# The experts' second product turned round: weights on the loaded side, in 64-column tiles

## The chip, the cores and the metric

One core of a Trainium2 chip runs the whole program, two transformer-like layers with a mixture of experts in the first. The metric is device time in microseconds, the median of several executions. The change touches one stage of it, the experts' two products.

## The reference, cut to what matters

```python
E, S, D, M = (48, 4, 256, 256);  K = D // S          # K = 64
def _L0_ffn_ref(x, Wr, W1, b1, W2, b2):
    xf = x.reshape(-1, D)                             # 4096 rows
    cap = int(CAP_FACTOR * T / E)                     # 128
    vals, idx = jax.lax.top_k((xf @ Wr.T).T, cap)
    w = jax.nn.softmax(vals, axis=-1)
    xg = xf[idx]
    h = jax.nn.gelu(jnp.einsum('ecd,esdm->ecsm', xg, W1) + b1[:, None], approximate=False)
    y = jnp.einsum('ecsm,esmk->ecsk', h, W2) + b2[:, None]
    y = y.reshape(E, cap, D) * w[..., None]
    out = jnp.zeros_like(xf).at[idx.reshape(-1)].add(y.reshape(-1, D))
```

Each of 48 experts takes 128 of the 4096 rows. In each of its four splits it multiplies them by a 256 x 256 matrix, applies gelu, and multiplies by a 256 x 64 matrix. The four results side by side make 256 columns. They get the bias b2, are weighed per row, and are added back at the rows they came from. Everything here is fp32.

## The kernel before

The stage is the second half of `expert_choice`. Each engine has its own program, a loop over the 48 experts e, and semaphores join them. The orders are written out by hand.

**SP** loads the weights into a ring of 8 slots: `load_expert` issues W1 (1024 KB), W2 (256 KB) and b2, which it spreads over all 128 partitions (128 KB). The loads of expert e+8 go out when `y_biased` says that add(e) is done.

**POOL** runs `scatter(e)`, then `gather(e+5)` (LEAD is 5), then waits until scatter(e-1) has landed and raises `y_free`. `scatter(e)` waits for `y_ready`, which weigh(e) raises. A gather is an indirect DMA of 128 rows of 1 KB, a scatter the same with an addition.

**TensorE**, in iteration e, runs up(e+1), turn(e+2), at some experts a small product for the list search (`pick_ps`), and down(e).
- `turn` transposes the gathered rows `xg` into `x_ps`, two transposes (L1216).
- `up` is the first product, 16 matmuls in the code (L1225), with loaded weights of 128 columns and 128 streamed columns.
- `down` is the second product (L1236). The loaded side is `act_h` (128 rows of the expert as columns), the streamed side is w2 with 64 columns:

```python
for s in range(S):
    cols = slice(s * KS, (s + 1) * KS)
    for c in range(KD):
        last = pe.matmul(y_ps[:, e % 2, cols], act_h[:, e % 2, s * KD + c, :], w2[:, e % RING, s, c, :], ...)
```

Each fp32 product of the code is two matmuls in the profile, and a transpose is one, so up has 32 records per expert, down 16 and turn 2.

**ScalarE**, in iteration e, runs gelu(e+1) (eight activations, L942), weigh(e) (L949) and x_copy(e+3) (L936). At e = 8 and e = 24 it also runs `exps`, one exponential for the list search (L953), for which it loads another table and then the gelu table again.

**VectorE** runs add(e) (L1106), which adds b2 to `y_ps`, and at about half of the experts pieces of the list search for later experts: rounds of top-8, a sort, counts and shifts.

PSUM has eight banks. x_ps takes one, h_ps four, y_ps (two buffers) one, and pick_ps two.

Of the kernel before, what the change touches and what calls it, by code (L numbers as in the profile page):

```python
# [12 lines left out]
ALU = mybir.AluOpType  # L13
ACT = mybir.ActivationFunctionType
# [6 lines left out]
P = 128  # L21
B, N, D = 4, 1024, 256
# [3 lines left out]
KD = D // P  # L26
# [4 lines left out]
KS = D // S  # L31
# [41 lines left out]
def columns(ap):  # L73

    return ap.rearrange("(c p) -> p c", p=P)
# [522 lines left out]
def expert_choice(nc, mk, g, a):  # L598

    with ExitStack() as ctx:  # L600
        t = Maker(nc, ctx)
        w1 = t.sb("w1", [P, RING, S, KD, M])
        w2 = t.sb("w2", [P, RING, S, KD, KS])
        b2_rows = t.sb("b2_rows", [P, RING, D])
        b1T = t.sb("b1T", [P, E * S, KD])
        index = t.sb("index", [P, E], U32)
        weight = t.sb("weight", [P, E])
# [6 lines left out]
        def load_expert(eng, e, q):  # L614

            eng.dma_start(w1[:, q], a["L0_ffn_W1"][bass.ds(e, 1)].rearrange("a s (p k) m -> p (a s) k m", k=KD)).then_inc(w_in[q], 16)
            eng.dma_start(w2[:, q], a["L0_ffn_W2"][bass.ds(e, 1)].rearrange("a s (p k) n -> p (a s) k n", k=KD)).then_inc(w_in[q], 16)
            eng.dma_start(b2_rows[:, q, :], a["L0_ffn_b2"][bass.ds(e, 1)].rearrange("a s n -> (a s n)").partition_broadcast(P)).then_inc(w_in[q], 16)

        lists_in = [mk.sem("lists_in0"), mk.sem("lists_in1")]  # L620
        proj2 = t.sb("proj2", [MF, 2, DH])
# [173 lines left out]
        with ExitStack() as c2:  # L795
# [3 lines left out]
            xg = t.sb("xg", [P, XG, D])  # L799
            xT = t.sb("xT", [P, 2, KD, P])  # L800
            act_h = t.sb("act_h", [P, 2, S * KD, P])
            y, biased_y = t.sb("y", [P, 2, D]), t.sb("biased_y", [P, 2, D])
            x_ps = t.ps("x_ps", [P, 2, D])
            h_ps = t.ps("h_ps", [P, 2, S * KD, P])
            y_ps = t.ps("y_ps", [P, 2, D])
            pick_ps = t.ps("pick_ps", [P, 2, 512])
            fold_ps = h_ps[:].rearrange("p q c n -> p (q c n)")

            top, at, at_f = t.sb("top", [P, CAP]), t.sb("at", [P, CAP], U32), t.sb("at_f", [P, CAP])
# [17 lines left out]
                mk.sem("slot_set"), mk.sem("xg_turned"), mk.sem("xT_ready"), mk.sem("up_done"),  # L827
                mk.sem("gelu_done"), mk.sem("down_done"), mk.sem("y_ready"))
            added = [mk.sem("added_even"), mk.sem("added_odd")]
            carried, y_free, y_biased = mk.sem("pool_carried"), mk.sem("y_free"), mk.sem("y_biased")  # L830
            mod_in, cols_in, w2_summed = mk.sem("mod1_in"), mk.sem("cols_in"), mk.sem("w2_summed")
            fold_turned, fold_copied, fold_done, fold_ready, blank = (
                mk.sem("fold_turned"), mk.sem("fold_copied"), mk.sem("fold_done"), mk.sem("fold_ready"), mk.sem("features_blank"))
# [10 lines left out]
            with nc.Block() as block:  # L844
                @block.sync
                def _(sp):
                    for e in range(FOLD_SLOT):
                        load_expert(sp, e, e)
                    sp.dma_start(g.b1_elu[:], columns(a["L1_attn_b1"]), allow_slow_non_contiguous=True).then_inc(cols_in, 16)
                    for i, name in enumerate(("ln1_g", "ln1_b")):  # L850
                        sp.dma_start(g.ln1_col[:, i, :], columns(a[f"L1_attn_{name}"]), allow_slow_non_contiguous=True).then_inc(cols_in, 16)
                    mod_columns = g.mod_dram[1].rearrange("b (s k p) -> s k p b", s=6, k=KD)
                    for k in range(KD):
                        sp.dma_start(g.gain_col[:, k, :], mod_columns[CB, k], allow_slow_non_contiguous=True).then_inc(cols_in, 16)
                        sp.dma_start(g.shift_col[:, k, :], mod_columns[SB, k], allow_slow_non_contiguous=True).then_inc(cols_in, 16)
                    for i, name in enumerate(("b1", "quantum_phases", "quantum_weights_real", "quantum_weights_imag")):
                        sp.dma_start(g.wav[:, i, :], columns(a[f"L1_ffn_{name}"]), allow_slow_non_contiguous=True).then_inc(cols_in, 16)
                    for i in range(2):
                        sp.wait_ge(fold_out[i], 16)
                        load_expert(sp, FOLD_SLOT + i, FOLD_SLOT + i)  # L860
                    sp.dma_start(mod[:, :, 0:GB, :], g.mod_dram[1].rearrange("b (s d) -> b s d", s=6)[:, 0:GB, :].partition_broadcast(P)).then_inc(mod_in, 16)
                    sp.wait_ge(elu_consts, 1)
                    for e in (ELU_SLOT, ELU_SLOT + 1):
                        load_expert(sp, e, e)
                    sp.wait_ge(wave_consts, 1)
                    load_expert(sp, WAVE_SLOT, WAVE_SLOT)
                    for e in range(E - RING):
                        sp.wait_ge(y_biased, e + 1)
                        load_expert(sp, e + RING, e % RING)
                    sp.wait_ge(mod_in, 16)  # L870
# [62 lines left out]
                def _(act):  # L933
# [10 lines left out]
                        last.then_inc(gelu_done, 1)  # L944

                    def weigh(e):
                        act.wait_ge(y_biased, e + 1)
                        act.wait_ge(y_free, e + 1)
                        act.activation(y[:, e % 2, :], biased_y[:, e % 2, :], ACT.Copy, scale=weight[:, e:e + 1]).then_inc(y_ready, 1)  # L949

                    def exps(p):
                        act.wait_ge(edge_ready, p + 1)
                        act.activation(ex[:], top[:], ACT.Exp, bias=edge[:, 1:2]).then_inc(top_exp, 1)  # L953
# [15 lines left out]
                    act.activation(g.elu_const[:], fold_ps[:, 0:CF], ACT.Copy)  # L969
                    act.activation(g.w2_sum[:], fold_ps[:, 512:512 + D], ACT.Copy)  # L970
                    act.wait_ge(wave_consts, 1)
                    act.activation(g.wave_const[:].rearrange("p c b -> p (c b)"), fold_ps[:, 1024:1024 + CF * B], ACT.Copy).then_inc(consts_out, 1)
                    exps(0)
                    act.sem_inc(y_ready, 2)
# [4 lines left out]
                    for e in range(E):  # L979
                        if e + 1 < E:  # L980
                            gelu(e + 1)
                        weigh(e)
                        if e + 3 < E:
                            x_copy(e + 3)
                        if e == COUNTS_AT[1]:
                            exps(1)
                        if e == COUNTS_AT[2]:
                            exps(2)

                @block.vector  # L990
                def _(dve):
# [14 lines left out]
                    def turn_back(p):  # L1006
                        dve.wait_ge(top_turned, p + 1)
                        v(dve.tensor_copy(topT[:].rearrange("p (q e) -> p q e", e=EP), of_pair(pick_ps[:, 1, 0:P], 1)))
                        dve.sem_inc(topT_ready, 1)
                        v(dve.tensor_copy(kept[:], pick_ps[0:HALF, 0, 0:P]))  # L1010

                    def sort(rows):

# [89 lines left out]
                    def add(e):  # L1103
                        dve.wait_ge(down_done, e + 1)
                        dve.wait_ge(y_ready, e + 1)
                        dve.tensor_tensor(biased_y[:, e % 2, :], y_ps[:, e % 2, :], b2_rows[:, e % RING, :], ALU.add).then_inc(y_biased, 1)  # L1106

                    v(dve.tensor_reduce(by_expert[:], g.ident[:].rearrange("p (n e) -> p e n", e=EP), AX.X, ALU.add))
                    v(dve.tensor_copy(same[:].rearrange("p (n e) -> p n e", e=EP), by_expert[:].unsqueeze(1).to_broadcast([P, LISTS, EP])))
# [63 lines left out]
                def _(pe):  # L1173
# [43 lines left out]
                        last.then_inc(turned, 1)  # L1217

                    def up(e):
                        pe.wait_ge(w_in[e % RING], 48 * (e // RING + 1))  # L1220
                        pe.wait_ge(xT_ready, e + 1)
                        for s in range(S):
                            for c in range(KD):
                                for k in range(KD):
                                    last = pe.matmul(h_ps[:, e % 2, s * KD + c, :], w1[:, e % RING, s, k, c::KD], xT[:, e % 2, k, :],  # L1225
                                                     start=(k == 0), stop=(k == KD - 1))
                        last.then_inc(up_done, 1)

                    def down(e):
                        pe.wait_ge(gelu_done, e + 1)  # L1230
                        if e:
                            pe.wait_ge(y_biased, e)
                        for s in range(S):
                            cols = slice(s * KS, (s + 1) * KS)
                            for c in range(KD):
                                last = pe.matmul(y_ps[:, e % 2, cols], act_h[:, e % 2, s * KD + c, :], w2[:, e % RING, s, c, :],  # L1236
                                                 start=(c == 0), stop=(c == KD - 1))
                        last.then_inc(down_done, 1)

                    pe.wait_ge(proj_in, 32)  # L1240
                    pe.transpose(fold_ps[:, 0:MF], proj2[:].rearrange("m i d -> m (i d)"), g.ident[0:MF, 0:MF]).then_inc(fold_turned, 1)
# [26 lines left out]
                    pe.wait_ge(wave_w_in, 16)  # L1268
                    for c in range(CF):
                        for k in range(KD):  # L1270
                            last = pe.matmul(fold_ps[:, 1024 + c * B:1024 + (c + 1) * B], w_wave[:, k, c * P:(c + 1) * P], g.shift_col[:, k, :],
                                             start=(k == 0), stop=(k == KD - 1))
                    last.then_inc(wave_consts, 1)
                    turn_top(0)
                    send_lists(0)
# [10 lines left out]
                    for e in range(E):  # L1286
                        if e + 1 < E:
                            up(e + 1)
                        if e + 2 < E:
                            turn(e + 2)  # L1290
                        for p in range(1, PHASES):
                            if e == COUNTS_AT[p] - 4:
                                turn_top(p)
# [12 lines left out]
                            if e == COUNTS_AT[p] + 5:  # L1306
                                join_weights(p)
                        down(e)
        mk.clear_signals()


# [1288 lines left out]
```

## Time and profile before

| | us |
|---|---|
| median of 3 executions (1674.59 to 1681.48) | 1678.65 |
| span of the profiled execution | 1681.8 |
| first up of the expert stage starts | 232.85 |
| last scatter of the expert stage is issued | 526.78 |
| TensorE busy, whole span | 1508.4 |
| DMA, whole span | 158.23 MB, mean 94 GB/s |

The span runs from the first to the last instruction of the profiled execution; it is one execution, so it need not be the median. A row of the timeline merges neighbours of one kind: it gives the start, the time to the end of the last, and their number. Matmuls overlap each other in the records: one of 0.27 us may be followed by the next 0.11 us later, so rates are read from starts. A time "to landing" runs from a DMA's issue to its last byte.

### The profile page before, as it was taken

The numbers are of one execution on the slowest core, as the hardware profiler recorded it, in microseconds if no ns is written. First come the engines' busy times: TensorE is split into PE (matmuls) and PEld (weight loads), VectorE is DVE, ScalarE is ACT, GpSimd is POOL, SyncE is SP. The second block draws the span as 40 slices with busy tenths as digits, with TensorE's granted clock in tenths as the row PEclk, the third lists the DMA queues.
The fourth block names the chain that finished last, engine by engine and source line by source line (L and its number), as shares of the span: only waits on it lengthen the run. The fifth ranks groups of instructions, "written<-read, shape, count | busy, mean of one in ns | idle before, by whom it ended". The sixth has DMA issues, their size and how long they took to land. (4 is left out here: it accounts for less than half of the span.)

```text
span 1681.8 us, 23213 instructions
## 1 busy us (share of the span) xinstructions
PE 1508.4 (90%) x8509; PEld 1261.0 (75%) x8509; DVE 1169.0 (70%) x2251; ACT 697.7 (41%) x1289; POOL 532.7 (32%) x520
## 2 busy tenths in 40 slices
PE   8876759999994699999987999999987899989997
PEld 7443649999994566666645888888866789979996
DVE  6674786674001778787638778787856888899996
ACT  1044124545442222222222333333326767767774
POOL 2412025555552022222314000000004555556666
PEclk9877569999997799999997999999998999999999
DMA  5545829999973101111013000000013100000001
GB/s 200 226 137 170 277 69 291 278 293 273 290 217 94 52 26 62 51 38 38 25 50 113 1 25 26 26 26 25 13 34 120 51 13 26 1 1 26 14 26 38
DMA packets 128624, 158.23 MB, mean 94 GB/s; under 512 B 14336, under 2 KB 96376, under 8 KB 127488
## 3 DMA queue, kind: packets, MB, share of 16 engines
q1 hardware_dynamic: 115296, 135.80, 24.9%
q0 software_dynamic: 9216, 12.59, 3.7%
q10 hardware_dynamic: 4000, 8.37, 1.4%
q8 instruction: 67, 1.10, 0.3%
q14 instruction: 45, 0.37, 0.1%
HBM read 122.35 MB, written 33.60 MB: 93 GB/s over the span
## 5 line engine op out<-in xcount | busy, mean ns | idle before, releaser
L2234 POOL TENSOR_TENSOR ff_hid_lo<-ff_hid,ff_hid_hi 128x512 fp32r<-128x512 f32 x128 | 172.7, 1353 | 148.2 <-ACT ff_hid_hi L2143 146.8
L1225 PE MATMUL h_ps<-xT,w 128*128 128x128 f32 x1536 | 192.9, 284 | 1.1 <-ACT xT L936 1.1
L1225 PEld LDWEIGHTS h_ps<-xT,w 128*128 128x128 f32 x1536 | 186.3, 197 | 1.7 <-issue 1.7
L2522 PE MATMUL ff_down<-ff_w_hi,ff_hid_hi 128*128 128x256 f32 x512 | 147.3, 288 | 7.6 <-POOL ff_hid_lo L2234 4.5
L2523 PE MATMUL ff_down<-ff_w_lo,ff_hid_hi 128*128 128x256 f32 x512 | 145.6, 284 | 0.0
L2524 PE MATMUL ff_down<-ff_w_hi,ff_hid_lo 128*128 128x256 f32 x512 | 145.6, 284 | 0.0
L116 POOL TENSOR_TENSOR ff_rstd<-ff_var,minus_half 128x4 f32<-128x4 f32 x24 | 26.0, 1083 | 360.3 <-DVE ff_var L111 356.2
L1106 DVE TENSOR_TENSOR biased_y<-y_ps,b_rows 128x256 f32<-128x256 f32 x48 | 20.4, 424 | 156.1 <-PE y_ps L1236 152.2
L1319 PE MATMUL k_ring<-w_hi,hT_hi 128*128 128x512 f32 x256 | 118.3, 462 | 9.9 <-DVE hT_lo L1479 6.4
L1660 PE MATMUL k_acc<-wide_rows,hk 128*128 128x512 f32 x256 | 119.6, 599 | 4.1 <-ACT wide_rows L1604 4.1
L1319 PE MATMUL q_ring<-w_hi,hT_hi 128*128 128x512 f32 x256 | 109.8, 429 | 8.8 <-PEq L99 6.8
L1949 PE MATMUL q_out_ps<-kv_sums,wide_rows 128*128 128x256 f32 x512 | 115.5, 379 | 0.0
L2522 PEld LDWEIGHTS ff_down<-ff_w_hi,ff_hid_hi 128*128 128x128 f32 x512 | 98.7, 193 | 14.8 <-POOL ff_hid_lo L2234 6.8
L1595 ACT ACTIVATE k_squares<-k_ring 128x1024 f32<-128x1024 f32 x32 | 32.8, 1025 | 182.0 <-PE k_ring L1321 182.0
L2508 PE MATMUL ff_ring<-ff_rowsT_hi,ff_w_hi 128*128 128x512 f32 x256 | 102.8, 402 | 4.6 <-DVE ff_hid L2328 2.8
L1949 PEld LDWEIGHTS q_out_ps<-kv_sums,wide_rows 128*128 128x128 f32 x512 | 96.3, 190 | 13.2
L942 ACT ACTIVATE act_h<-h_ps,b1T 128x128 f32<-128x128 f32 x384 | 104.2, 391 | 2.7 <-PE h_ps L1225 2.7
L1321 PE MATMUL k_ring<-w_hi,hT_lo 128*128 128x512 f32 x256 | 102.0, 399 | 0.0
L2509 PE MATMUL ff_ring<-ff_rowsT_lo,ff_w_hi 128*128 128x512 f32 x256 | 102.0, 399 | 0.0
L1320 PE MATMUL k_ring<-w_lo,hT_hi 128*128 128x512 f32 x256 | 101.9, 398 | 0.0
L2523 PEld LDWEIGHTS ff_down<-ff_w_lo,ff_hid_hi 128*128 128x128 f32 x512 | 98.9, 193 | 4.1
L1321 PE MATMUL q_ring<-w_hi,hT_lo 128*128 128x512 f32 x256 | 101.8, 398 | 0.0
(419 smaller groups left out, 3683.5 us busy)
## 6 DMA issues: line engine op xcount, KB each, us to landing
w<-in_L_ffn_W_dram SPq DMA_DIRECT2D x48, 1024.0 KB, 5.8
w<-in_L_ffn_W_dram SPq DMA_DIRECT2D x48, 256.0 KB, 6.0
expert_sum_dram<-f_zero SPq DMA_DIRECT2D x8, 1024.0 KB, 15.1
b_rows<-in_L_ffn_b_dram SPq DMA_DIRECT2D x48, 128.0 KB, 8.3
x<-in_L_attn_x_dram SPq DMA_DIRECT2D x4, 1024.0 KB, 12.0
h_dram<-hg SPq DMA_DIRECT2D x8, 512.0 KB, 3.0
hk<-expert_sum_dram SPq DMA_DIRECT2D x8, 512.0 KB, 4.2
hT_hi<-expert_sum_dram SPq DMA_DIRECT2D x8, 512.0 KB, 4.9
```

What stands on the lines that cost most here:

```text
L942: last = act.activation(act_h[:, e % 2, s * KD + c, :], h_ps[:, e % 2, s * KD + c, :], ACT.Gelu, bias=b1T[:, e * S + s, c:c + 1])
L1225: last = pe.matmul(h_ps[:, e % 2, s * KD + c, :], w1[:, e % RING, s, k, c::KD], xT[:, e % 2, k, :], start=(k == 0), stop=(k == KD - 1))
L1319: pe.matmul(out, x[0], w[0][:, cols], start=start, stop=False)
L1321: return pe.matmul(out, x[1], w[0][:, cols], start=False, stop=stop)
L1660: last = pe.matmul(acc[:, k, cols], hk[:, n % KV_RING, j, k * P:(k + 1) * P], dash[:, n % 2, j, cols], start=(j == 0), stop=(j == G - 1))
L1949: last = pe.matmul(out_ps[:, i % 2, 0:D], qnT[:, i % 2, c, :], kv_out(i // TB)[:, c, :], start=(c == 0), stop=(c == CH - 1))
L2234: pool.tensor_tensor(hid_lo[:, m % PARTS, :], hid[:, m % WHOLES, :], hid_hi[:, m % PARTS, :].bitcast(F32), ALU.subtract).then_inc(part_low, 1)
L2508: pe.matmul(slot(u), high[:, d, cols], x[:, n % 2, d, :], start=(d == 0), stop=False)
L2509: pe.matmul(slot(u), high[:, d, cols], x_low[:, n % 2, d, :], start=False, stop=False)
L2522: pe.matmul(into, hid_hi[:, m % PARTS, tile], high[:, c, :], start=(c == 0 and j % 2 == 0), stop=False)
L2523: pe.matmul(into, hid_hi[:, m % PARTS, tile], low[:, c, :], start=False, stop=False)
L2524: last = pe.matmul(into, hid_lo[:, m % PARTS, tile], high[:, c, :], start=False, stop=(c == CF - 1 and j % 2 == 1))
```

## The change

- The second product is turned round. The loaded side is now w2, 64 columns; the streamed side is `act_h`, 128 columns. The result `yT_ps` is transposed: splits 0 and 1 of a pair lie in partitions 0 to 63 and 64 to 127, and the two pairs side by side. In program order neighbours alternate between the two halves.
- b2 lies along partitions then. It is loaded once (`b2_rows`, 48 x 256), transposed by two small products at the start and copied to `b2T`. The 48 loads that spread b2 are gone, and up waits for 32 instead of 48.
- add(e) adds a column of `b2T` to `yT_ps` and writes `yT`.
- A new step back(e) on TensorE transposes `yT` into `y_ps`. weigh(e) reads `y_ps` and waits for `y_back`.
- The order: back(e-1) stands after turn(e+2) and ahead of down(e); weigh(e-1) stands after gelu(e+1), so one iteration later than before. back(47) and weigh(47) follow the loops.
- `yT_ps` and `y_ps` have one buffer each, in banks of their own, and pick_ps shrinks to one bank. In `turn_back` the copy to `kept` moves ahead of the signal.

```diff
@@ load_expert
-            eng.dma_start(b2_rows[:, q, :], a["L0_ffn_b2"][bass.ds(e, 1)].rearrange("a s n -> (a s n)").partition_broadcast(P)).then_inc(w_in[q], 16)
@@ SP
+                    sp.dma_start(b2_rows[:], a["L0_ffn_b2"].rearrange("e s n -> e (s n)")).then_inc(b2_in, 16)
@@ ScalarE
                     def weigh(e):
-                        act.wait_ge(y_biased, e + 1)
+                        act.wait_ge(y_back, e + 1)
                         act.wait_ge(y_free, e + 1)
-                        act.activation(y[:, e % 2, :], biased_y[:, e % 2, :], ACT.Copy, scale=weight[:, e:e + 1]).then_inc(y_ready, 1)
+                        act.activation(y[:, e % 2, :], y_ps[:], ACT.Copy, scale=weight[:, e:e + 1]).then_inc(y_ready, 1)
...
                     act.wait_ge(wave_consts, 1)
+                    act.activation(b2T[:], fold_ps[:, 1536:1536 + KD * E].rearrange("p (k e) -> p k e", k=KD), ACT.Copy)
...
                     for e in range(E):
                         if e + 1 < E:
                             gelu(e + 1)
-                        weigh(e)
+                        if e:
+                            weigh(e - 1)
                         if e + 3 < E:
                             x_copy(e + 3)
...
+                    weigh(E - 1)
@@ VectorE
                         v(dve.tensor_copy(topT[:].rearrange("p (q e) -> p q e", e=EP), of_pair(pick_ps[:, 1, 0:P], 1)))
+                        v(dve.tensor_copy(kept[:], pick_ps[0:HALF, 0, 0:P]))
                         dve.sem_inc(topT_ready, 1)
-                        v(dve.tensor_copy(kept[:], pick_ps[0:HALF, 0, 0:P]))
...
                     def add(e):
                         dve.wait_ge(down_done, e + 1)
                         dve.wait_ge(y_ready, e + 1)
-                        dve.tensor_tensor(biased_y[:, e % 2, :], y_ps[:, e % 2, :], b2_rows[:, e % RING, :], ALU.add).then_inc(y_biased, 1)
+                        if e == 0:
+                            dve.wait_ge(consts_out, 1)
+                        dve.tensor_tensor(yT[:, e % 2], yT_ps[:], b2T[:, :, e:e + 1].to_broadcast([P, KD, P]), ALU.add).then_inc(y_biased, 1)
@@ TensorE
-                        for s in range(S):
-                            cols = slice(s * KS, (s + 1) * KS)
+                        for pair in range(S // 2):
                             for c in range(KD):
-                                last = pe.matmul(y_ps[:, e % 2, cols], act_h[:, e % 2, s * KD + c, :], w2[:, e % RING, s, c, :],
-                                                 start=(c == 0), stop=(c == KD - 1))
+                                for i in range(2):
+                                    s = 2 * pair + i
+                                    last = pe.matmul(yT_ps[i * KS:(i + 1) * KS, pair, :], w2[:, e % RING, s, c, :], act_h[:, e % 2, s * KD + c, :],
+                                                     start=(c == 0), stop=(c == KD - 1))
                         last.then_inc(down_done, 1)
+
+                    def back(e):
+                        pe.wait_ge(y_biased, e + 1)
+                        pe.wait_ge(y_ready, e + 2)
+                        for k in range(KD):
+                            last = pe.transpose(y_ps[:, k * P:(k + 1) * P], yT[:, e % 2, k, :], g.ident[:])
+                        last.then_inc(y_back, 1)
...
                         if e + 2 < E:
                             turn(e + 2)
+                        if e:
+                            back(e - 1)
```

## Rows read from the trace of the kernel before

**Rows 1.** The page, section 1: busy time, share, matmuls.

```profile
PE 1508.4 (90%) x8509; PEld 1261.0 (75%) x8509; DVE 1169.0 (70%) x2251; ACT 697.7 (41%) x1289; POOL 532.7 (32%) x520
```

**Rows 2.** Windows: stretch, its length, busy per engine, granted clock, DMA share, GB/s.

```profile
500.00:520.00 20.00, 20.00 (x175) 20.00 (x174) 1.61 (x4) 9.57 (x34) 8.16 (x11) 1.00 0.21 31
```

**Rows 3.** Timeline of one expert: start, us, engine, line, operation, tiles, count.

```profile
453.47 3.99 PE L1225 MATMUL h_ps<-xT,w 128*128 128x128 f32 x32
453.67 0.42 DVE L1106 TENSOR_TENSOR biased_y<-y_ps,b_rows 128x256 f32<-128x256 f32 x1 [5.36 <-PE y_ps L1236]
...
454.22 0.57 ACT L949 ACTIVATE y<-biased_y,weight 128x256 f32<-128x256 f32 x1
...
457.29 0.39 PE L1216 MATMUL x_ps<-ident,xg 128*128 128x128 f32 x2
...
457.44 1.02 POOL L888 DMA_INDIRECT xg<-h_dram,slot  x1
457.52 1.90 PE L1236 MATMUL y_ps<-w,act_h 128*128 128x64 f32 x16
457.72 0.38 ACT L936 ACTIVATE xT<-x_ps 128x256 f32<-128x256 f32 x1 [2.93 <-PE x_ps L1216]
458.00 2.17 ACT L942 ACTIVATE act_h<-h_ps,b1T 128x128 f32<-128x128 f32 x8
...
459.25 3.99 PE L1225 MATMUL h_ps<-xT,w 128*128 128x128 f32 x32
```

**Rows 4.** Waits, 243 to 525 us: waiter, releaser, us in total, times, longest.

```profile
DVE biased_y L1106 <- PE y_ps L1236: 150.1, 36, 5.4
```

**Rows 5.** Timeline of TensorE at two experts with narrow list products.

```profile
275.34 0.43 PE L1183 MATMUL pick_ps<-flip,topT 128*64 128x128 f32 x2
...
281.36 0.39 PE L1216 MATMUL x_ps<-ident,xg 128*128 128x128 f32 x2
281.67 0.62 PE L1189 MATMUL pick_ps<-order,picks 64*32 64x128 f32 x4
282.23 2.00 PE L1236 MATMUL y_ps<-w,act_h 128*128 128x64 f32 x16
284.06 3.98 PE L1225 MATMUL h_ps<-xT,w 128*128 128x128 f32 x32
```

**Rows 6.** DMA view, 440 to 485 us: queues' share of 16 engines, gathers' landing.

```profile
q1 hardware_dynamic: 9479, 11.28, 80.2%
q0 software_dynamic: 1531, 2.09, 20.9%
...
xg<-h_dram,slot POOLq DMA_INDIRECT x8, 6.0
```

**Rows 7.** The same view, 360 to 400 us.

```profile
q1 hardware_dynamic: 7545, 9.21, 72.9%
q0 software_dynamic: 1152, 1.57, 17.7%
...
xg<-h_dram,slot POOLq DMA_INDIRECT x7, 4.9
```

**Rows 8.** Timeline of ScalarE around the exponential at e = 8.

```profile
301.79 1.28 ACT L953 ACT_TABLE_LOAD   x1
...
304.79 2.18 ACT L942 ACTIVATE act_h<-h_ps,b1T 128x128 f32<-128x128 f32 x8
306.81 0.56 ACT L949 ACTIVATE y<-biased_y,weight 128x256 f32<-128x256 f32 x1
```

**Rows 9.** Timeline of TensorE: the turn of expert 13.

```profile
312.97 0.39 PE L1216 MATMUL x_ps<-ident,xg 128*128 128x128 f32 x2
```

**Rows 10.** Timeline of the stage's end.

```profile
520.87 1.90 PE L1236 MATMUL y_ps<-w,act_h 128*128 128x64 f32 x16
...
523.38 1.97 PE L1236 MATMUL y_ps<-w,act_h 128*128 128x64 f32 x16 [0.61 <-ACT act_h L942]
...
525.84 0.51 ACT L949 ACTIVATE y<-biased_y,weight 128x256 f32<-128x256 f32 x1 [2.07 <-DVE biased_y L1106]
```

More of the change, by code:

```diff
@@ L603, in expert_choice @@
         w2 = t.sb("w2", [P, RING, S, KD, KS])
-        b2_rows = t.sb("b2_rows", [P, RING, D])
+        b2_rows, b2T = t.sb("b2_rows", [E, D]), t.sb("b2T", [P, KD, E])
         b1T = t.sb("b1T", [P, E * S, KD])
@@ L801, in expert_choice @@
             act_h = t.sb("act_h", [P, 2, S * KD, P])
-            y, biased_y = t.sb("y", [P, 2, D]), t.sb("biased_y", [P, 2, D])
+            y, yT = t.sb("y", [P, 2, D]), t.sb("yT", [P, 2, KD, P])
             x_ps = t.ps("x_ps", [P, 2, D])
             h_ps = t.ps("h_ps", [P, 2, S * KD, P])
-            y_ps = t.ps("y_ps", [P, 2, D])
-            pick_ps = t.ps("pick_ps", [P, 2, 512])
+            yT_ps, y_ps = t.ps("yT_ps", [P, KD, P]), t.ps("y_ps", [P, D])
+            pick_ps = t.ps("pick_ps", [P, 2, 2 * P])
             fold_ps = h_ps[:].rearrange("p q c n -> p (q c n)")
@@ L829, in expert_choice @@
             added = [mk.sem("added_even"), mk.sem("added_odd")]
-            carried, y_free, y_biased = mk.sem("pool_carried"), mk.sem("y_free"), mk.sem("y_biased")
+            carried, y_free, y_biased, y_back = mk.sem("pool_carried"), mk.sem("y_free"), mk.sem("y_biased"), mk.sem("y_back")
+            b2_in = mk.sem("b2_in")
             mod_in, cols_in, w2_summed = mk.sem("mod1_in"), mk.sem("cols_in"), mk.sem("w2_summed")
@@ L1219, in up @@
                     def up(e):
-                        pe.wait_ge(w_in[e % RING], 48 * (e // RING + 1))
+                        pe.wait_ge(w_in[e % RING], 32 * (e // RING + 1))
                         pe.wait_ge(xT_ready, e + 1)
@@ L1270, in _ @@
                         for k in range(KD):
-                            last = pe.matmul(fold_ps[:, 1024 + c * B:1024 + (c + 1) * B], w_wave[:, k, c * P:(c + 1) * P], g.shift_col[:, k, :],
-                                             start=(k == 0), stop=(k == KD - 1))
+                            pe.matmul(fold_ps[:, 1024 + c * B:1024 + (c + 1) * B], w_wave[:, k, c * P:(c + 1) * P], g.shift_col[:, k, :],
+                                      start=(k == 0), stop=(k == KD - 1))
+                    pe.wait_ge(b2_in, 16)
+                    for k in range(KD):
+                        last = pe.transpose(fold_ps[:, 1536 + k * E:1536 + (k + 1) * E], b2_rows[:, k * P:(k + 1) * P], g.ident[0:E, 0:E])
                     last.then_inc(wave_consts, 1)
@@ L1308, in _ @@
                         down(e)
+                    back(E - 1)
         mk.clear_signals()
```

## The prediction

> **What bounds the kernel now.** The page first: TensorE is busy for 90% of the span [rows 1]. That is an average over stages, so I cut out the stage that the diff touches, the 48 experts, from about 233 to 527 us. By the windows view TensorE is busy 20.00 of 20.00 us there, at a granted clock of 1.00 (the 2.4 GHz level), even where DMA has almost stopped [rows 2]. The timeline shows one expert [rows 3]: up from 453.47 to 457.29 (3.82 us), turn to 457.52 (0.23), down to 459.25 (1.73). The period is 5.78 us, nothing idle. The waits view agrees from the other side: VectorE's add waited for down 36 times, 150 us in all, so VectorE isn't the bound [rows 4]. ScalarE does about 3.1 us of work per expert [rows 3]. TensorE's own work sets the stage, so what the change does to its instructions is paid 48 times, unless a new wait is longer.
>
> Down has 8 products in the code and 16 matmuls in its row: each fp32 product runs as two passes. A pass of down takes 1.73 / 16 = 0.11 us though it streams only 64 columns, as long as a pass of turn that streams 128. So today down is held by loading 128 columns of weights per pass, not by streaming.
>
> **Down, turned round.** There are still 8 products, so 16 passes. Each loads 64 columns and streams 128. The load halves, the streaming doubles, and nothing is won unless products in the two column halves run side by side. No row of before shows neighbours in different halves. The nearest are the list products in narrow shapes [rows 5]: four passes with 32-column weights, all in one place, fill 0.56 us with the change of shape, so about 0.11 us each. The two passes with 64-column weights last 0.43 us together; less one matmul's 0.27 that is 0.16 between their starts, which I read as 0.05 of loading and 0.11 of streaming. Three values follow for the 16 passes:
> - one after another: 16 x 0.11 = 1.76 us
> - side by side, but issued strictly in order: a product's second pass streams together with the next product's first, whose load starts only when that second pass has been issued. Each product then costs 0.16: 8 x 0.16 = 1.28 us
> - side by side with the loads early: two passes in 0.11: 0.88 us
>
> I take the middle: loads in the rows never start before the pass ahead of them has been issued, and that order alone doesn't forbid two halves at once. Both ends go into the range. The page "TensorEngine Tiling (Array Packing)" of the Trainium skill, under Key Properties, says that different tiles can load and multiply in parallel; no run here shows it yet.
>
> **The change of shape.** Turn and up use the whole array, down now half of its columns. The rows have the price [rows 5]. Going in: from turn to the narrow product 0.31 us where turn to down takes 0.23, so 0.08. Coming out: the four passes take 0.56 where 4 x 0.11 = 0.44 would do, and the down behind them 1.83 instead of 1.73, so 0.22. Together 0.30 us per expert. The same page of the Trainium skill speaks against the change here: it says that changing the tiling mode drains TensorE; the gaps just read agree. Without that price every sum below would be some 14 us lower.
>
> Down becomes 1.28 + 0.30 = 1.58 us instead of 1.73.
>
> **Back.** Two more transposes, the form of turn: 0.23 us [rows 3]. Net per expert -0.15 + 0.23 = +0.08, period 5.86, and 48 x 0.08 = **+3.8 us**. Its two waits are met: add(e-1) ends early in up(e+1), and weigh(e-2) ran one up earlier. Behind back in TensorE's order stands down(e), which waited for the same add anyway.
>
> **VectorE and ScalarE.** The add reads as many elements of PSUM as before (0.42 us); weigh reads PSUM instead of SBUF, 0.57 us either way in my sum. Both hide under up.
>
> **The b2 loads.** 48 issues on SP and 128 of 1664 KB per expert go. DMA was no wait of TensorE, so this gives nothing directly. It matters through the gathers: in the late stretch the 16 engines are 80.2 + 20.9 = 101% taken and a gather lands after 6.0 us [rows 6]; at 73 + 18 = 91% it takes 4.9 us [rows 7]. Without b2 the first becomes 80.2 x 1280/1408 + 20.9 = 94%, over a period of 5.86 some 92%, and I take 5.1 us.
>
> **What becomes late: the gathers.** This is the moved step. weigh(e) used to follow down(e) at once, at 454.22. Now back(e) comes after up(e+2), and on ScalarE weigh(e) is queued behind gelu(e+2), which ends at 458.00 + 2.17 = 460.17, 2.88 us after that up's end. So weigh is later by 5.9 us. POOL issues scatter(e) and then gather(e+5), both behind weigh(e): the gather is issued 457.44 - 454.22 = 3.22 us after weigh's start [rows 3]. turn(e+5) stands two periods after up(e+2)'s end. So a gather has 2 x 5.86 - 2.88 - 3.22 = 5.62 us to land. The median of 5.1 fits. Before, 5.4 us were over: the gather at 457.44 landed at 463.4, two periods after 457.29 is 468.85. But gathers scatter by a microsecond or more about their medians, and each one over 5.62 stops TensorE by its excess. For some 33 experts at 0.1 us on average I put **+3 us**.
>
> At two experts ScalarE loads tables for exps and back, and its gelu ends late: 304.79 + 2.18 [rows 8]. weigh(8) will stand behind that gelu, at 306.81, so gather(13) lands at 306.81 + 3.22 + 5.1 = 315.1, while turn(13) is at 312.97 [rows 9] + 2 x 0.08. Wait 2.0 us, twice: **+4 us**.
>
> **Both ends of the stage.** The last two experts: down(46) now ends at 520.87 + 0.23 + 1.58 = 522.7, back(46) needs weigh(45), which follows the gelu that ended before 523.4, so 523.8; down(47) ends near 525.7, then add, back, and weigh(47) at about 526.7 instead of 525.84 [rows 10]. **+1 us.** At the start, two small transposes, one copy, and a copy of 0.28 ahead of the signal that releases the list product: **+0.3 us**; the loads of b2_rows hide under the first list search.
>
> **Sum:** 3.8 + 3 + 4 + 1 + 0.3 = 12.1; 1681.8 + 12.1 = 1693.9. The median of before is 3.1 below the profiled span, so **1691 us**.
>
> **Rivals.**
> - *No overlap of the halves.* Down is 1.76 + 0.30 = 2.06: +0.33 + 0.23 = +0.56 per expert, 26.9 us. The period of 6.34 leaves gathers 6.58 us, so only the two table places wait, 1 us each; the ends 2.3. Together 31: **1710 us**. For it: no row shows overlap, and streaming at 0.11 us is all that the narrow rows show. Against it: they never change halves. Chance 0.35.
> - *Full overlap, gathers take the bound.* Down is 0.88 + 0.30 = 1.2, period 5.48 by TensorE alone, but the gathers would have 4.86 us at a DMA share near 95 to 97%, where they need 5.3 to 5.5. So the period settles near 5.7. That gains some 2.6 us, the ten longer experts with list products gain 3, the table places take 5, the ends 0.6: **1679 us**, no change. Chance 0.15.
> - *The other side: full overlap, and gathers that land in under 4.86 us* because b2's packets are gone. Then 48 x 0.30 = 14.4 is gained and 5 given back: **1669 us**. It is decided by the gathers' median: rows 7 show 4.9 at 91%, so it needs a queue that b2 alone made long. Chance 0.07.
> - *Each step from one half to the other costs like a change of shape*, 0.2 us and more, eight times per expert: 1710 + 77 = 1787 us. Chance 0.03. The Trainium skill's page on tiling, Key Properties, ties the drain to the mode, not to the tile; that speaks against it.
> - The forecast: 0.38; 0.02 for what I don't see.
>
> **The numbers.** 0.5% of this kernel is 8.4 us, about what a measurement can tell from no change. The forecast lies 12 above, and its own range is 1684 to 1698: of its 0.38, 0.30 is slower by over 0.5% and 0.08 within. With 0.35, 0.03 and a remainder of 0.01, slower has 0.69. Full overlap lies within, except 0.02: with 0.08, the 0.13 and 0.01 that makes 0.22. Faster: 0.07 + 0.02 = 0.09. The range, 1676 to 1714, takes in both ends of down's price and leaves out the last two named rivals.
>
> **What the profile after would show.** In the middle of the stage: from the first matmul of down to the next up 1.6 us (2.1 without overlap, 1.2 with all of it); 2 more transposes per expert at 0.23; a step of 0.1 to 0.2 us at each change of shape. The gather's issue 3.2 us after weigh, and weigh right behind gelu. turn's matmuls waiting for DMA of xg, longest at two places near 313 and 410 us. The add and weigh themselves never waited for. The prediction is wrong if down is 2.0 us or more, if gathers no longer depend on DMA share and land in 3 us or in 7, or if VectorE's list work comes to hold the adds.

## The result, and the profile after

The changed kernel takes 1691.3 us (median of 7, 1684.6 to 1694.3) where the kernel before takes 1679.5 (median of 7). The ratio is 1.0072, 95% interval 1.0052 to 1.0092: slower by 12 us. The prediction said 1691. The number is right, but two groups of its terms are wrong, by 20 and by 17 us, in opposite directions. One execution of `b2_loads_back`, a run below, took 2995 us, in the slow state, and is left out of that run's median.

The page of the changed kernel, section 1; it answers to [rows 1]:

```profile
PE 1492.8 (89%) x8607; PEld 1227.4 (73%) x8607; DVE 1168.4 (69%) x2251; ACT 693.7 (41%) x1290; POOL 532.1 (32%) x520
```

TensorE is busy for 16 us less, in a kernel that takes longer. Here is one expert in the timeline of the changed kernel; it answers to [rows 3]:

```profile
452.51 0.40 PE L1222 MATMUL x_ps<-ident,xg 128*128 128x128 f32 x2
...
452.74 0.38 PE L1251 MATMUL y_ps<-ident,yT 128*128 128x128 f32 x2
...
453.05 1.09 PE L1243 MATMUL yT_ps<-act_h,w 128*64 128x128 f32 x16
453.22 2.17 ACT L943 ACTIVATE act_h<-h_ps,b1T 128x128 f32<-128x128 f32 x8
...
454.08 4.04 PE L1231 MATMUL h_ps<-xT,w 128*128 128x128 f32 x32
...
455.21 0.54 ACT L950 ACTIVATE y<-y_ps,weight 128x256 f32<-128x256 f32 x1
...
458.40 1.01 POOL L889 DMA_INDIRECT xg<-h_dram,slot  x1
459.06 0.31 PEld L1222 LDWEIGHTS x_ps<-ident,xg 128*128 128x128 f32 x2 [1.14 <-DMA xg<-h_dram,slot]
459.06 0.50 PE L1222 MATMUL x_ps<-ident,xg 128*128 128x128 f32 x2 [0.95 <-DMA xg<-h_dram,slot]
```

From the start of back to the start of down it takes 0.31 us, where two transposes take 0.23, and from there to the next up 1.03. So down, with both changes of shape around it, takes 0.31 - 0.23 + 1.03 = 1.11 us, where it took 1.73. Its row is 1.09 us long and one matmul 0.27, so the 16 passes start within 0.82 us, 0.055 us apart on average. Back adds 0.23. Then the next turn, at 459.06, waits 0.95 us for its gathered rows. weigh stands behind gelu, and the gather goes out 3.2 us after weigh (458.40 against 455.21), as predicted.

The waits view, 243 to 530 us of the changed kernel (waiter, releaser, us in total, times, longest). In the kernel before no turn waited for a gather:

```profile
DVE yT L1112 <- PE yT_ps L1243: 155.3, 36, 8.3
...
PE x_ps L1222 <- DMA xg<-h_dram,slot: 16.3, 10, 4.2
PEld h_ps L1231 <- issue: 8.3, 45, 0.3
PEld yT_ps L1243 <- issue: 6.2, 35, 0.3
```

The first row is VectorE waiting for down, as in [rows 4]; that costs nothing. The second is the new one: TensorE waited 16.3 us in ten waits for gathered rows. The last two rows are gaps of the weight loads, 0.3 us at most, at the changes of shape.

The longest waits stand where the prediction put them, behind the two exponentials, and they cost more than themselves. The timeline of the first of them, POOL's issue of the gather and then TensorE:

```profile
306.06 1.01 POOL L889 DMA_INDIRECT xg<-h_dram,slot  x1 [0.15 <-POOL pool_spare L878]
...
313.11 0.70 PE L1222 MATMUL x_ps<-ident,xg 128*128 128x128 f32 x2 [4.16 <-DMA xg<-h_dram,slot]
...
314.41 1.98 PE L1243 MATMUL yT_ps<-act_h,w 128*64 128x128 f32 x16
316.31 5.22 PE L1231 MATMUL h_ps<-xT,w 128*128 128x128 f32 x32
```

and its windows view (stretch, length, busy time of the engines, granted clock, DMA share, GB/s), beside the one that answers to [rows 2]:

```profile
300.00:320.00 20.00, 15.49 (x121) 14.43 (x120) 9.38 (x36) 9.01 (x30) 9.29 (x15) 0.83 0.66 184
...
500.00:520.00 20.00, 20.00 (x196) 18.82 (x195) 1.70 (x4) 11.08 (x40) 11.07 (x18) 1.00 0.31 51
```

The gather was issued at 306.06 and turn could start at 313.11, so its rows took 7.0 us to land. After the wait of 4.16 us down takes 1.98 instead of 1.09 and the next up 5.22 instead of 4.04: the granted clock fell to the lower of its levels, 1.2 GHz, for part of that stretch, and the mean over the window is 0.83. The wait at 417.39 (3.97 us) has an up of 4.55 behind it, and that of 265.97 (2.12) one of 5.15. From 500 us on the weight loads are over, and a gather lands in 2.8 us (median of four). There turn waits for nothing, and the same kernel does 196 matmuls in 20 us; the kernel before did 175.

The end of the stage, timeline of the changed kernel; it answers to [rows 10]:

```profile
529.83 1.09 PE L1243 MATMUL yT_ps<-act_h,w 128*64 128x128 f32 x16
...
531.45 0.44 PE L1251 MATMUL y_ps<-ident,yT 128*128 128x128 f32 x2 [0.53 <-DVE yT L1112]
...
533.63 0.47 ACT L950 ACTIVATE y<-y_ps,weight 128x256 f32<-128x256 f32 x1 [3.22 <-POOLq L929]
```

The last weigh's input was there at 531.45 + 0.44 = 531.9, and it started 1.7 us later. L929 is POOL's wait for the scatter two experts back, which frees y.

### The profile page after: what moved, and what is told of

Read it like the earlier page. It is cut to its first block and busy times, and to the rows that moved or that the text cites. A ratio compares the mean times of both kernels' runs of the same rounds, so it can differ in the third digit from the quotient of the medians.

```text
span 1686.2 us, 23411 instructions
## 1 busy us (share of the span) xinstructions
PE 1492.8 (89%) x8607; PEld 1227.4 (73%) x8607; DVE 1168.4 (69%) x2251; ACT 693.7 (41%) x1290; POOL 532.1 (32%) x520
## 3 DMA queue, kind: packets, MB, share of 16 engines
q8 instruction: 68, 1.11, 0.3%
## 5 line engine op out<-in xcount | busy, mean ns | idle before, releaser
L1231 PE MATMUL h_ps<-xT,w 128*128 128x128 f32 x1536 | 198.2, 289 | 1.1 <-ACT xT L937 1.1
L1112 DVE TENSOR_TENSOR yT<-yT_ps,b2T 128x256 f32<-128x256 f32 x48 | 20.4, 424 | 164.8 <-PE yT_ps L1243 157.7
L1340 PE MATMUL q_ring<-w_lo,hT_hi 128*128 128x512 f32 x256 | 101.2, 395 | 0.0
## 6 DMA issues: line engine op xcount, KB each, us to landing
expert_sum_dram<-f_zero SPq DMA_DIRECT2D x8, 1024.0 KB, 14.9
```

Of the source, the lines that this page charges most:

```text
L1340: pe.matmul(out, x[0], w[1][:, cols], start=False, stop=False)
```

## The experiments

Each run was timed beside the kernel before on the same chip, in two groups on two chips: the four runs from lead6 to halves_grouped, where the median of before was 1678.5 us, and the four from halves_by_two on, where it was 1675.4. So runs of different groups are compared by their ratios; a ratio is not exactly the quotient of the two medians. "Stage" is from the first up's start to the last scatter's issue in the one profiled execution, read from the views of the tiles. It leaves out the rest of the kernel, which took between 1375.8 and 1387.9 us in the ten profiles, in no order that follows the edits: a difference of medians holds some microseconds of that.

| run | median us | ratio to before, 95% interval | stage us | turn waits for xg, us | down to next up, median us |
|---|---|---|---|---|---|
| before | 1679.5 | | 293.9 | 0 | 1.73 |
| changed | 1691.3 | 1.0072 (1.0052 to 1.0092) | 304.4 | 16.3 | 1.02 |
| lead6 | 1665.1 | 0.9914 (0.9891 to 0.9938) | 280.7 | 0 | 1.02 |
| weigh_first | 1661.3 | 0.9912 (0.9882 to 0.9943) | 277.9 | 0 | 1.02 |
| old_weigh_late | 1705.8 | 1.0138 (1.0097 to 1.0179) | 320.1 | 14.9 | 1.73 |
| halves_grouped | 1680.8 | 1.0019 (1.0002 to 1.0036) | 298.6 | 0 | 1.51 |
| halves_by_two | 1663.8 | 0.9933 (0.9907 to 0.9958) | 282.6 | 0 | 1.07 |
| b2_loads_back | 1694.8 | 1.0118 (1.0048 to 1.0187) | 310.0 | 20.5 | 1.02 |
| old_lead6 | 1676.9 | 1.0001 (0.9979 to 1.0023) | 294.5 | 0 | 1.73 |
| lead6_weigh_first | 1661.4 | 0.9918 (0.9893 to 0.9944) | 278.1 | 0 | 1.02 |

### Gathers one expert earlier

```diff
-            XG, LEAD = 8, 5
+            XG, LEAD = 8, 6
```

> The changed kernel, but gathers issued six experts ahead instead of five. Theory A, late gathers hold the period and TensorE's own work would allow 5.44 us: turn's waits for xg (16 us in all) and the slow clock behind the two longest go, so about 1670 us, 20 below the changed kernel and 9 below the one before. Theory B, the loss is TensorE's own extra work (back, the gaps at changes of shape): within 3 us of the changed kernel, 1691 us. Theory C, with a period of 5.44 us the weight loads become late: turn no longer waits, up does, and the time lies between, near 1682 us.

Theory A holds: 26 us below the changed kernel, and 14 below the kernel before. TensorE's timeline shows the period, 5.44 us, with no wait in it:

```profile
457.39 1.09 PE L1243 MATMUL yT_ps<-act_h,w 128*64 128x128 f32 x16
458.41 4.04 PE L1231 MATMUL h_ps<-xT,w 128*128 128x128 f32 x32
462.29 0.39 PE L1222 MATMUL x_ps<-ident,xg 128*128 128x128 f32 x2
462.52 0.38 PE L1251 MATMUL y_ps<-ident,yT 128*128 128x128 f32 x2
462.83 1.09 PE L1243 MATMUL yT_ps<-act_h,w 128*64 128x128 f32 x16
```

The turned product itself is therefore a gain. Theory C fails: up never waits for its weights. The shorter period does show another wait: TensorE waits 1.9 us once for the list search on VectorE, where the longest such wait in the kernel before was 1.0.

### The weighing ahead of gelu

```diff
                     for e in range(E):
+                        if e:
+                            weigh(e - 1)
                         if e + 1 < E:
                             gelu(e + 1)
-                        if e:
-                            weigh(e - 1)
```

> The changed kernel with five ahead as it is, but on ScalarE weigh(e-1) stands ahead of gelu(e+1) instead of behind it, which issues each gather some 2.2 us earlier. Theory A: most waits of turn for xg go, about 1673 us. Theory B: 1691 us, or more if the later gelu holds down.

Another edit at the same wait, and again it goes: three short waits of the loads are left, 0.8 us. It is better than expected by 12 us, and most of that was my pricing: I left out what the slow clock had cost and the end of the stage. The stage is 26.5 us shorter than in the changed kernel, and 16.3 of waits, 8 of slow clock and 1.7 at the end make 26; the rest of the 30 us between the medians lies outside the stage. Gathers land later here than in the changed kernel (6.7 against 5.8 us in the stretch from 360 to 400), and it doesn't matter.

### The moved weighing alone, in the kernel before

```diff
                         if e + 1 < E:
                             gelu(e + 1)
-                        weigh(e)
+                        if e:
+                            weigh(e - 1)
...
+                    weigh(E - 1)
```

> The kernel before with one thing of the change: weigh(e-1) in the iteration of gelu(e+1), one expert later. The second product stays as it was. Theory A: two periods must hold 2.9 + 3.2 + 5.9 us, so 6.0 us per expert instead of 5.78 for some 33 experts (+7), two stalls of 3 to 4 us at the exponentials with a slow clock behind each (+8), and the later end (+2): near 1695 us. Theory B, lateness costs nothing because gathers have slack: 1680 us.

1705.8 us, 11 above what theory A said, and against theory B. The sign and place are theory A's: turn waits 14.9 us. The waits view, 243 to 535 us:

```profile
PE x_ps L1218 <- DMA xg<-h_dram,slot: 14.9, 12, 4.6
```

The waits and the later end were about as expected. What was too small was again the clock. Two rows of its TensorE timeline, the longest wait and the up behind it:

```profile
426.06 0.70 PE L1218 MATMUL x_ps<-ident,xg 128*128 128x128 f32 x2 [4.63 <-DMA xg<-h_dram,slot]
...
430.28 6.15 PE L1227 MATMUL h_ps<-xT,w 128*128 128x128 f32 x32
```

An up of 6.15 us instead of 3.99. So the one reordered line costs the old kernel 26 us of stage, where the whole change costs 10.5.

### The kernel before with gathers earlier

> The kernel before with gathers six ahead. Theory A: its gathers had 5 us to spare, so nothing is gained, 1678.5 us within 3. If it gains, late gathers were a cost before too and the gain of six ahead says less about the change.

The edit is that of lead6, in the kernel before. Ratio 1.0001, and the interval allows 0.2% either way: no gain. Lateness of gathers is a cost of the change, not one that was there before, so lead6's gain isn't borrowed from elsewhere.

### Both together

> The changed kernel with gathers six ahead and weigh(e-1) ahead of gelu(e+1). Theory A: either alone removed the waits for xg, so together they give nothing more in the middle, and only the earlier last weigh (2 to 3 us at the stage's end): 1661 to 1664 us. Rival, both gather chains were still losing: below 1657 us.

A ratio of 0.9918 and a stage of 278.1 us, as weigh_first alone (0.9912 and 277.9): the wait is gone once, and can't go twice.

### The order of the halves

In lead6, the eight products in another order: all four of the lower half, then the upper (halves_grouped), or two and two (halves_by_two, where the loop over i stands between those over pair and c). The edit of halves_grouped:

```diff
-                        for pair in range(S // 2):
-                            for c in range(KD):
-                                for i in range(2):
+                        for i in range(2):
+                            for pair in range(S // 2):
+                                for c in range(KD):
                                     s = 2 * pair + i
```

> The changed kernel with gathers six ahead, and the eight products of down in another order: the four of the lower half, then the four of the upper half, so that neighbours share a half. Theory of the overlap (two halves stream side by side only where neighbours differ): down goes from 1.03 back to about 1.8 us, period 6.2, some 35 us above the run with six ahead alone. Rival, 0.065 us a pass comes from the shorter loads: down stays near 1.0 us and the time within 3 us of the run with six ahead.

> The changed kernel, gathers six ahead, products of down in blocks of two per half: lower, lower, upper, upper. Theory W, TensorE starts a later product of the free half while up to four passes of the other half are still to come (that is what the records of the grouped order show at its one border): down stays near 1.1 us, the time near the run with six ahead, 1665 us. Rival, strictly in order (a pass may only overlap its direct neighbour): down about 1.4 us, 18 us above that run, 1683 us.

TensorE's timeline of halves_grouped, then of halves_by_two:

```profile
457.77 1.58 PE L1243 MATMUL yT_ps<-act_h,w 128*64 128x128 f32 x16
459.28 4.04 PE L1231 MATMUL h_ps<-xT,w 128*128 128x128 f32 x32
```

```profile
445.97 1.14 PE L1243 MATMUL yT_ps<-act_h,w 128*64 128x128 f32 x16
447.04 4.04 PE L1231 MATMUL h_ps<-xT,w 128*128 128x128 f32 x32
```

Same products, same loads, another order: 1.51 us instead of 1.02, and 16 us on the median. The smaller loads alone give nothing: within one half the passes start 0.11 us apart, as they did before. So the gain is the overlap of the two halves. But grouped down isn't the 1.8 us I expected, so the 35 us didn't come: 0.49 us more per expert would be 23, and the stage grew by 18. The longer period takes up part of what lead6 still loses on the way: its waits of TensorE in the stage add up to 7.6 us, here to 4.2, and 3.4 us of its stage ran at the lower clock, here none. The windows view of halves_grouped, with the matmuls of L1243 alone, cuts that down in three (stretch, length, busy, matmuls that touch it, clock, DMA):

```profile
457.77:458.26 0.49, 0.49 (x4) 1.00 0.98 359
458.26:458.65 0.39, 0.39 (x10) 1.00 1.02 332
458.65:459.13 0.48, 0.48 (x9) 1.00 1.06 309
```

In 0.49 us at the start 4 matmuls are touched, in the 0.39 us in the middle 10. A matmul that lasts 0.27 us is counted in each stretch that it touches; of one half, with 0.11 us between starts, no more than 7 could touch the middle. So both halves run there: the upper one began before the lower was through, in an order that puts all of the lower first. The starts alone say the same: they lie within 1.58 - 0.27 = 1.31 us, and 16 passes one after another at 0.11 would need 1.6 at least. Blocks of two keep nearly all of the overlap (1.07 against 1.02 us, ratios 0.9933 against 0.9914), so theory W holds and the strictly ordered rival, with 1.4 us, fails.

### The b2 loads put back

```diff
             eng.dma_start(w2[:, q], ...).then_inc(w_in[q], 16)
+            eng.dma_start(b2_wide[:, q, :], a["L0_ffn_b2"][bass.ds(e, 1)].rearrange("a s n -> (a s n)").partition_broadcast(P)).then_inc(w_in[q], 16)
```

> The changed kernel (five ahead) with the 48 spreading loads of b2 put back, into a tile that nobody reads. Theory of the prediction, a gather's landing time follows the DMA share: landing about 0.5 us later, 0.25 us per expert, two longer stalls: about 1700 us. Rival, landing depends on the 1 MB load that is under way and not on b2: 1691 us as without.

In this run up waits for 48 again, as in the kernel before. It isn't settled by the times: 1.0118, from three executions, with an interval that covers the changed kernel's whole interval. The profiles lean to a small cost: turn waits 20.5 us instead of 16.3, and the stage is 5.6 us longer. But a gather lands 5.7 us after its issue instead of 5.4 (medians of all 48; in the kernel before it was 5.6), 0.3 us and not the 0.5 that my reading of [rows 6, 7] gave. That reading was weak from the start. The DMA view of the changed kernel, 440 to 485 us, then 360 to 400:

```profile
q1 hardware_dynamic: 8453, 10.45, 75.0%
q0 software_dynamic: 1502, 2.02, 22.2%
...
xg<-h_dram,slot POOLq DMA_INDIRECT x8, 5.7
```

```profile
q1 hardware_dynamic: 7074, 8.58, 70.6%
q0 software_dynamic: 1335, 1.82, 22.0%
...
xg<-h_dram,slot POOLq DMA_INDIRECT x7, 5.8
```

At 93% a gather takes 5.8 us and at 97% 5.7. With rows 7, 4.9 us at 91%, the share alone doesn't tell the landing time.

## Why the prediction was right, point by point

1. **TensorE's own work bounds the stage: right, once the gathers are in time.** In lead6 no turn waits, and the period is TensorE's 5.44 us; halves_grouped lengthens down alone by 0.49 us, and the time follows. In the changed kernel itself ten turns were held by gathers.

2. **Down at 1.28 + 0.30 us: wrong, the term was 0.41 us too large.** Measured, with the changes of shape, it is 1.11 us and 0.06 us that the next up takes longer (3.88 instead of 3.82), 1.17 in all. The step that failed is "I take the middle: loads in the rows never start before the pass ahead of them has been issued". Those rows showed neighbours in one place of the array only. Between two halves a pass starts while earlier ones of the other half are still to come (halves_grouped). The price of 0.16 us per product was also a misreading: the distance of 0.16 us stands once, behind the change of shape, and not in each product. The windows view of the changed kernel, the matmuls of L1243 alone:

```profile
453.05:453.21 0.16, 0.16 (x2) 1.00 1.27 371
453.21:453.32 0.11, 0.11 (x4) 1.00 1.07 317
```

Two matmuls start in the first 0.16 us and no third. The rows don't name the halves; in program order the two are the first pass of each. From then on each half starts one every 0.11 us: 0.16 + 6 x 0.11 = 0.82 us from the first start to the last, as measured. The third value of my list, 0.88 us, was the true one. Over 48 experts the step is 20 us.

3. **The change of shape at 0.30 us: right.** Into it 0.31 - 0.23 = 0.08; 1.03 - 0.88 = 0.15 for down's late second passes and the way out of it, and 0.06 in the next up. 0.29 in all.

4. **Back at 0.23: right.** Its waits were met but for a few: 0.35 and 0.24 us for weigh at the table places, 1.58 us for the first add, where down(1) had waited 1.2 before, and 1.48 us for weigh(45) at the end, which the prediction had seen. TensorE's period alone is 5.44 us; the prediction had 5.48 for full overlap. 48 x 0.34 = 16 us are gained.

5. **weigh later by 5.9 us, gathers late: right in mechanism, too small.** old_weigh_late shows the mechanism by itself, and lead6 and weigh_first take it away. The prediction had 3 + 4 us of waits; with the shorter period there is less time for a gather, 2 x 5.44 - 6.1 = 4.8 us, while the median gather took 5.4 and not 5.1, and ten waits made 16.3. The two places at the exponentials cost 4.16 and 3.97 us, where I had 2.0 each: their gathers landed after 7.0 and 6.6 us, where I had put in the median.

6. **The clock: missing.** Mean granted clock from 240 to 520 us is 0.97, and was 1.00: 280 x 0.03 = 8 us. No term of the sum had it. The granted clock was at the lower level during or just behind the four longest waits (2.12, 4.16, 2.28 and 3.97 us; the mean is 0.91 in 260 to 280 us and in 340 to 360, and 0.83 in 300 to 320), and not at the six others, which were under 1 us.

7. **The ends: +1 us, measured 1.7.** From the last turn to the last scatter it takes 13.4 us instead of 11.7. The prediction left out that the last weigh also waits for the scatter two experts back. The +0.3 us at the start wasn't measured.

Together -16 (4) + 16.3 (5) + 8 (6) + 1.7 (7) = 10 us, and the stage grew by 304.4 - 293.9 = 10.5 us. The forecast's terms gave 12: down and back 20 us too dear, the waits with the clock 16.3 + 8 - 7 = 17 us too cheap. The two errors aren't independent: a shorter down leaves the gathers less time, so what it gains comes back as waiting. That a missing clock term and a down that was too dear cancelled to within 2 us is luck all the same, and so is the median's last microsecond or two, which the rest of the kernel moves.

The rival "full overlap, gathers take the bound" had the mechanism, with a chance of 0.15, and its 1679 us was 12 too low for points 5 and 6. The forecast's own mechanism, a half overlap with few waits, didn't happen. The rival of the other side asked for gathers under 4.86 us; they took 5.4.

## What to carry to other kernels

When a step on one engine is moved by an iteration, follow what is queued behind it on the other engines, and give the transfer at the end of that chain as many more iterations of lead as the step was moved. Here one constant, LEAD, turned this change from 12 us slower to 14 faster. Price a long wait of TensorE with the slow matmuls behind it: here 16.3 us of waiting brought 8 more. And when a change has a gain and a loss on different engines, time each alone: old_weigh_late has the loss without the gain, lead6 the gain without the loss.

## What the runs showed of the hardware that I had not expected

Matmuls of fp32 in the two column halves of the array overlap fully: 16 passes of 128 columns at 0.055 us each, 0.88 us in all, where one half alone needs 0.11 each. And they don't start in program order. The order of halves_grouped and its 1.31 us above show it. A second place is in the changed kernel's timeline, where the list product L1189 (two passes, lower half) stands ahead of down in the program:

```profile
274.21 0.32 PE L1189 MATMUL pick_ps<-flip,topT 128*64 128x128 f32 x1
274.22 0.32 PE L1243 MATMUL yT_ps<-act_h,w 128*64 128x128 f32 x1
274.37 0.27 PE L1189 MATMUL pick_ps<-flip,topT 128*64 128x128 f32 x1
274.38 1.13 PE L1243 MATMUL yT_ps<-act_h,w 128*64 128x128 f32 x15
```

A matmul of down starts 0.01 us after L1189's first pass and 0.15 before its second. I take it for one of the upper half, since L1189 holds the lower one, though the row doesn't name the half; the first of these stands in the program behind both passes of L1189 and behind down's own first product. The page "TensorE: Matmul & The Clock Gate" of the Trainium skill, Part 3, says that matmuls start and end in program order; for starts in different halves these rows and the grouped order say otherwise. How far ahead TensorE looks was tested with the blocks of two and four above only.
